# Identity turns that nobody reads, put into TensorE's stops behind conv3, in the end phase and ahead of the first expert tile

## The chip, the cores and the metric

One core of one Trainium2 chip runs the kernel. The metric is the device time of one execution in microseconds (us), and of several runs the median. Profiles come from one execution that the hardware profiler recorded; its span runs from the first to the last instruction.

## The reference, cut to what matters

A residual bottleneck of three convolutions, linear attention, and a mixture of eight experts, all in float32, on 16 images of 256 channels and 14 x 14 pixels (3136 tokens of 256 features).

```python
# 1. convolutions; _bn takes mean and variance over all images and pixels
out = jax.nn.relu(_bn(_conv(x, w1, b1, 1, 0), g1, be1))      # 256 -> 64, 1x1
out = jax.nn.relu(_bn(_conv(out, w2, b2, 1, 1), g2, be2))    # 64 -> 64, 3x3
out = _bn(_conv(out, w3, b3, 1, 0), g3, be3)                 # 64 -> 256, 1x1
x = jax.nn.relu(x + jax.nn.softplus(residual_scale)[0] * out)
t = _to_tokens(x)                                            # (16, 196, 256)
# 2. linear attention on the normalised tokens, 16 heads of 16
q = jax.nn.softmax(q * SCALE, axis=-1); k = jax.nn.softmax(k, axis=-2)
context = jnp.einsum('bnd,bne->bde', q, k)
t = t + jnp.einsum('bde,bnd->bne', context, v).reshape(...) @ w_out + b_out
# 3. experts on the normalised tokens: the two best of eight, weighted
probs = jax.nn.softmax(flat @ gate_w + gate_b, axis=-1)
top_p, top_i = jax.lax.top_k(probs, 2)
for e in range(8):
    h = jax.nn.gelu(flat @ w1[e] + b1[e], approximate=False)  # 256 -> 1024
    out = out + comb[:, e:e + 1] * (h @ w2[e] + b2[e])        # 1024 -> 256
```

The transposes ("turns") that the change adds compute nothing of this: they turn the constant identity matrix, and no instruction reads where they write.

## The kernel before

Every engine has its own instruction list, written by hand in its own block, and runs it in order; engines meet at counted semaphores (`wait_ge(s, n)` waits until semaphore s has reached n). `wait_for(engine, stage, other, name, i)` is such a wait for step `name` of image i. TensorE writes into `ps`, eight banks of 512 float32 columns.

**Convolutions (to about 60 us).** Each layer is computed in 8 chunks of two images (392 columns, `CW`), a chunk per bank. conv3 has two halves of 128 channels, so 16 chunks through 8 banks (L751). Batch norm needs statistics of all chunks before any can go on: VectorE takes them (L1106, counted in `s_st3`), ScalarE copies each chunk behind them into `img` (L533, counted in `s_ca`), and VectorE works out the coefficients (L1038 to L1061). Between conv1 and conv2, and between conv2 and conv3, TensorE runs 22 and 16 products that nobody reads (`spare_products`, L730); they go into columns 392 to 511 of bank `SPARE` (4). Behind conv3 there are none.

**Attention and routing (60 to about 283 us).** A loop over the 16 images runs stages one behind the other: `in` (batch norm and ReLU on VectorE and ScalarE, then `in_turn`, L763, turns the image to tokens by rows), `norm` (statistics, `norm_xT`, L775), `qkv` (L785, L796), `soft`, `ctx`, `out`, `norm2` (L864), gate logits (L874), and for each pair of images the routing on VectorE and `route_rank` on TensorE (L884 to L889), which gives every token its row in its experts' lists. GpSimd scatters the token rows there (L456). The code behind the loop, here the end phase, writes out the last images' steps by hand. There TensorE sums the counts of tokens per expert (L922, L931), VectorE makes from them the table of tiles (L1336 to L1392, its steps counted in `s_tab`), and ScalarE and TensorE wait for parts of it (`TAB_ROWS`, `TAB_EXPERTS`).

**Experts (from about 283 us).** 56 tiles of 128 token rows go through a pipeline over slots. ScalarE loads a tile's rows (`load_rows`, L666); TensorE turns them (`x_turn`, L940); ScalarE and VectorE split them into a leading and a rest part (L672, L1522); TensorE multiplies them by the first matrix in two halves of six products (`hidden`, L947); VectorE adds the bias (L1537), ScalarE takes the GELU (L677); TensorE turns the result (`h_turn`, L974), it is split again (L683, L1516), and TensorE multiplies by the second matrix (`expert_out`, L947). Tiles overlap: in slot m TensorE does `h_turn` of tile m-2, `x_turn` of tile m, `hidden` of tile m-1 and `expert_out` of tile m-2; ScalarE issues the third load of rows only behind the GELU and the copy of the first tiles.

Of the kernel before, what the change touches and what calls it, by code (L numbers as in the profile page):

```python
# [36 lines left out]
CHUNKS = 8  # L37
CW = 2 * HW
# [14 lines left out]
SPARE = 4  # L53
# [27 lines left out]
LAST = B - 1  # L81
# [6 lines left out]
def after(stage, engine, name, i):  # L88

    steps = STEPS[stage][engine]  # L90
    return i * len(steps) + steps.index(name) + 1


def moe_block(nc, x, w1t, w2t, w3t, norms, res_scale, wqkv, wout, bout, gate_w, gate_b, ew1, ew2, eb, out):
# [5 lines left out]
    with ctx:  # L100
        def sb(name, shape, dt=F32):
            return ctx.enter_context(nc.sbuf_tensor(name, shape, dt))

        def sem(name):
            return ctx.enter_context(nc.semaphore(name))
# [15 lines left out]
        ident = sb("ident", [128, 128])  # L121
# [89 lines left out]
        ps = ctx.enter_context(nc.psum_tensor("ps", [128, 8, 512], F32))  # L211
# [11 lines left out]
        s_st3 = sem("conv3_stats")  # L223
        s_fin = sem("conv_coefficients")
        s_ca = sem("conv_applied")
# [43 lines left out]
        def wait_for(eng, stage, engine, name, i):  # L269

            if i >= 0:
                eng.wait_ge(S[stage][engine], after(stage, engine, name, i))
# [441 lines left out]
        def _(pe):  # L714
# [11 lines left out]
            def spare_products(layer, times):  # L726

                pe.wait_ge(s_cst, STATS_READ[layer])
                for _ in range(times):
                    last = pe.matmul(ps[:, SPARE, CW:512], w1s[:, 0, :], img[:, 0, 0:512 - CW], start=True, stop=True)  # L730
                last.then_inc(s_spare, 1)

            pv = pad[:, :].rearrange("p (b r c) -> p b r c", b=B, c=16)
            spare_products(0, 22)
            pe.wait_ge(s_wl, 1)
# [11 lines left out]
            for c in range(CHUNKS):  # L747
                for h in range(2):
                    n = 2 * c + h
                    pe.wait_ge(s_ca, CHUNKS + n + 1 if n < 8 else 2 * CHUNKS + n - 7)  # L750
                    pe.matmul(ps_chunk(n % 8), w3s[:, h * 128:(h + 1) * 128], mid2[:, c * CW:(c + 1) * CW],  # L751
                              start=True, stop=True).then_inc(s_conv, 1)
            pe.wait_ge(s_wa, 9 * 16)
            pe.wait_ge(s_const, NCONST)
            pe.wait_ge(s_ca, 4 * CHUNKS)
# [95 lines left out]
            def norm2_xT(i):  # L851
                wait_for(pe, "norm2", "act", "norm1", i)
                bank = psL
                if i < LAST:
                    wait_for(pe, "gate", "act", "xT", i - 1)
                else:
                    bank = psT
                    wait_for(pe, "ctx", "act", "proj", LAST - 1)

                if i % 2 == 0:  # L860
                    wait_for(pe, "route", "vec", "bias", i // 2 - 1)
                for k in range(2):
                    for j in range(2):
                        last = pe.transpose(bank[:, k * HW + j * HALF:k * HW + (j + 1) * HALF],  # L864
                                            rows[:, i % RING, j, k * 128:(k + 1) * 128], ident[0:HALF, 0:HALF])
                last.then_inc(S["norm2"]["pe"], 1)

            def norm2_logits(i):
                wait_for(pe, "gate", "act", "xT", i)
                wait_for(pe, "route", "vec", "bias", i // 2 - 1)  # L870
                for j in range(2):
                    at = CW + ((i % 2) * 2 + j) * E
                    for k in range(2):
                        last = pe.matmul(psL[0:HALF, at:at + E], xT2[:, i % 2, k, j * HALF:(j + 1) * HALF],  # L874
                                         gw[:, k, :], start=(k == 0), stop=(k == 1))
                last.then_inc(S["gate"]["pe"], 1)

            def route_rank(g):

                both = rt[:, BOTH[g % 2]]  # L880
                wait_for(pe, "route", "vec", "both", g)
                wait_for(pe, "place", "vec", "pos", g - 1)
                wait_for(pe, "norm", "act", "xT", min(2 * g + ROUTE_LAG, B - 1))
                pe.matmul(psX[0:HALF, CW:CW + 32], upper[:, :], both.rearrange("p t e -> p (t e)"),  # L884
                          start=True, stop=False)
                for t in range(3):
                    pe.matmul(psX[0:HALF, CW + (t + 1) * E:CW + 32], ones[:, 0:HALF],
                              both[:, t:t + 1, :].to_broadcast([HALF, 3 - t, E]), start=False, stop=False)
                pe.matmul(psX[0:HALF, CW:CW + 32], ones[:, 0:HALF],  # L889
                          run[:, g % 2, :].unsqueeze(1).to_broadcast([HALF, 4, E]),  # L890
                          start=False, stop=True).then_inc(S["route"]["pe"], 1)
# [30 lines left out]
            pe.matmul(psV[:, E:2 * E], ones[:, :], run[:, (G - 1) % 2, :], start=True, stop=True)  # L922
            norm2_xT(LAST - 2)
            norm2_logits(LAST - 2)
            norm2_xT(LAST - 1)
            norm2_xT(LAST)
            norm2_logits(LAST - 1)
            norm2_logits(LAST)
            route_rank(G - 1)
            wait_for(pe, "route", "vec", "run", G)  # L930
            pe.matmul(psV[:, 0:E], ones[:, :], run[:, (G + 1) % 2, :], start=True, stop=True).then_inc(s_cntp, 1)  # L931
            route_rank(G)

            def x_turn(i, b, late):

                pe.wait_ge(s_xr[b], (i // XR + 1) * 16 if isinstance(i, int) else late)
                if not isinstance(i, int) or i >= 1:
                    pe.wait_ge(s_xlo, i)
                for k in range(2):
                    last = pe.transpose(ps[:, 0, k * 128:(k + 1) * 128], xr[:, b, k * 128:(k + 1) * 128], ident[:, :])  # L940
                last.then_inc(s_eT, 1)
# [42 lines left out]
                         lambda k: off + W2HI + k * C, W2LO - W2HI, C).then_inc(s_yp, 1)  # L984

            pe.wait_ge(s_tab, TAB_EXPERTS)

            def pe_slot(m, b, before=None, e=None, late=None):

                st, p = isinstance(m, int), b % 2  # L990
                if before is None:
                    e = expert_of(m - 1) if 0 <= m - 1 < SLOTS else None
                    before = expert_of(m - 2) if m >= 2 else None
                if not st or 0 <= m - 2 < SLOTS:
                    h_turn(m - 2, p)
                if m == 1:
                    hidden(0, 0, e)
                if not st or m < SLOTS:
                    x_turn(m, b, late)
                if m != 1 and e is not None:  # L1000
                    hidden(m - 1, 1 - p, e)
                if not st or 0 <= m - 2 < SLOTS:
                    expert_out(m - 2, p, before)
# [642 lines left out]
```

## Time and profile before

| | us |
|---|---|
| median of 3 runs | 687.7 (687.45 to 690.37) |
| profiled execution, whole | 689.3 |
| its span, first to last instruction | 687.4 |
| mean granted TensorE clock | 0.947 of full |
| TensorE busy (PE) | 616.8 (90% of the span) |
| VectorE busy (DVE) | 455.4 (66%) |
| ScalarE busy (ACT) | 319.2 (46%) |
| GpSimd busy (POOL) | 218.5 (32%) |

PE stands for TensorE's products and turns, PEld for its weight loads, DVE for VectorE, ACT for ScalarE, POOL for GpSimd, ACTq and SPq for transfers issued by ScalarE and SyncE. L947 is line 947 of the kernel before. A timeline row gives the start, the time, the engine, the line, the operation, what it writes and reads, the number of merged instructions, and in brackets how long the engine had been idle before it and which instruction released it. Busy time of TensorE is modelled at the ends, since its instructions overlap; where something is compared closely, starts are compared with starts. The granted clock is given as a share of 2.4 GHz.

### The profile page before, as it was taken

The page shows a single profiled execution, that of the slowest core. Times are in us where ns is not written, and L with a number is a line of the kernel's source. Part 1 is how long each engine was busy: PE and PEld are TensorE (multiplying, and loading weights), DVE is VectorE, ACT ScalarE, POOL GpSimd, SP SyncE. Part 2 cuts the span into 40 slices and gives each one's busy share as a digit, 9 for nine tenths or more (in the row PEclk, how much of TensorE's full clock was granted, in tenths as well). Part 3 has the DMA queues.
Part 4 walks back from the last instruction along what each step waited for, and adds up shares of the span by engine and source line. Part 5 has one row for each costly group of instructions (what it writes and reads, how often), then busy time and mean ns, then how long its engine had stood idle before and what let it go on. Part 6 is the DMA issues. An engine that isn't in the chain of part 4 may idle for free.

```text
span 687.4 us, 13862 instructions
## 1 busy us (share of the span) xinstructions
PE 616.8 (90%) x3960; PEld 546.7 (80%) x3960; DVE 455.4 (66%) x1472; ACT 319.2 (46%) x624; POOL 218.5 (32%) x194
## 2 busy tenths in 40 slices
PE   7984799989999974489999999999999999999982
PEld 3862678878788864379999999999999999999971
DVE  2877899999998886346565655556565655656550
ACT  0575788888785522133334333333334333333430
POOL 7041233315656667502112222222121222212120
PEclk9996899999999985599999999999999999999995
DMA  9718999888959953422383745626528337222211
GB/s 247 239 62 306 361 351 326 302 293 302 353 201 361 355 182 92 132 45 38 73 289 49 232 131 162 200 44 196 171 35 291 76 99 256 48 44 37 32 17 16
DMA packets 50198, 121.10 MB, mean 176 GB/s; under 512 B 7309, under 2 KB 38865, under 8 KB 43985
## 3 DMA queue, kind: packets, MB, share of 16 engines
q1 hardware_dynamic: 30368, 98.54, 39.8%
q0 software_dynamic: 11136, 14.00, 12.0%
q10 hardware_dynamic: 8624, 7.68, 4.2%
q8 instruction: 39, 0.64, 0.4%
q14 instruction: 31, 0.25, 0.1%
HBM read 68.09 MB, written 52.11 MB: 175 GB/s over the span
## 4 chain that ended last, share of the span: by engine, by line
PE 69%; DVE 20%; issue 4%; ACT 2%; POOL 2%; DMA 1%; DVEq 1%; SPq 0%; ACTq 0%; POOLq 0%
PE ps L947 46%; PE ps L974 7%; DVE wset L1225 3%; DVE stt L1134 2%; PE ps L740 2%; PE ps L722 2%; PE ps L796 2%; PE ps L940 2%; PE ps L751 2%; PE ps L785 1%; PE ps L847 1%; POOL rows_by_expert L456 1%; DVE tc L1125 1%; DVE img L1219 1%; DVE cT L1211 1%
## 5 line engine op out<-in xcount | busy, mean ns | idle before, releaser
L478 POOL DMA_INDIRECT out<-ys,xr x56 | 86.7, 1548 | 302.4 <-DVE ys L1548 220.5
L947 PE MATMUL ps<-wset,hTh 128*128 x896 | 162.7, 282 | 3.4 <-DVE hTl L1516 3.4
L947 PE MATMUL ps<-wset,xrTh 128*128 x448 | 148.7, 414 | 1.2 <-DVE xrTl L1522 1.2
L947 PEld LDWEIGHTS ps<-wset,hTh 128*128 128x128 f32 x896 | 141.6, 190 | 9.7 <-issue 4.8
L677 ACT ACTIVATE hb<-hb 128x512 f32<-128x512 f32 x112 | 70.3, 633 | 138.4 <-DVE hb L1537 133.0
L947 PE MATMUL ps<-wset,hTl 128*128 x448 | 126.1, 281 | 0.0
L683 ACT CAST hTh<-ps 128x512 fp32r<-128x512 f32 x112 | 60.2, 590 | 99.4 <-PE ps L974 99.4
L1543 DVE TENSOR_TENSOR yb<-ps,bset 128x256 f32<-128x256 f32 x56 | 23.8, 425 | 124.5 <-PE ps L947 124.5
L947 PEld LDWEIGHTS ps<-wset,xrTh 128*128 128x128 f32 x448 | 82.0, 193 | 17.7 <-issue 1.6
L947 PE MATMUL ps<-wset,xrTl 128*128 x224 | 90.2, 403 | 0.0
L1537 DVE TENSOR_TENSOR hb<-ps,bset 128x512 f32<-128x512 f32 x112 | 75.4, 684 | 19.7 <-PE ps L947 19.6
L947 PEld LDWEIGHTS ps<-wset,hTl 128*128 128x128 f32 x448 | 85.0, 190 | 0.0
L1516 DVE TENSOR_TENSOR hTl<-ps,hTh 128x512 fp32r<-128x512 f32 x112 | 71.8, 682 | 11.2 <-ACT hTh L683 8.3
L456 POOL DMA_INDIRECT rows_by_expert<-rows,slot x64 | 62.4, 975 | 23.5 <-issue 16.6
L432 POOL TENSOR_TENSOR img<-img,bo 98x512 f32<-98x512 f32 x16 | 29.2, 1828 | 100.2 <-ACT xh L551 96.0
L974 PE MATMUL ps<-ident,hb 128*128 128x128 f32 x448 | 58.2, 273 | 0.7 <-ACT hb L677 0.7
L796 PE MATMUL ps<-xT,wq 128*128 128x196 f32 x256 | 50.1, 339 | 8.9 <-ACT vT L573 8.2
L796 PEld LDWEIGHTS ps<-xT,wq 128*128 128x128 f32 x256 | 43.9, 194 | 14.3 <-ACT xT L568 6.8
L947 PEld LDWEIGHTS ps<-wset,xrTl 128*128 128x128 f32 x224 | 43.1, 193 | 10.5
L974 PEld LDWEIGHTS ps<-ident,hb 128*128 128x128 f32 x448 | 50.3, 141 | 0.9 <-ACT hb L677 0.9
L940 PE MATMUL ps<-ident,xr 128*128 128x128 f32 x112 | 22.1, 280 | 13.3 <-DMA xr<-rows_by_expert 13.3
L1225 DVE TENSOR_TENSOR wset<-wset 128x2048 fp32r<-128x2048 f32 x14 | 31.9, 2281 | 0.0
(199 smaller groups left out, 945.8 us busy)
## 6 DMA issues: line engine op xcount, KB each, us to landing
split_weights<-wset SPq DMA_DIRECT2D x16, 2048.0 KB, 7.4
wset<-split_weights SPq DMA_DIRECT2D x32, 1024.0 KB
wset<-in_ew SPq DMA_DIRECT2D x16, 1024.0 KB, 10.5
xr<-rows_by_expert ACTq DMA_DIRECT2D x56, 132.5 KB, 2.3
bset<-in_eb SPq DMA_DIRECT2D x8, 640.0 KB
out<-img SPq DMA_DIRECT2D x16, 196.0 KB
img<-in_x SPq DMA_DIRECT2D x6, 392.0 KB, 7.2
rows_by_expert<-padrow SPq DMA_DIRECT2D x9, 132.5 KB, 3.3
```

The costliest lines, as they stand in the source:

```text
L432: pool.tensor_tensor(t, t, bo2[:, :, :].rearrange("p j d -> p (j d)"), ALU.add).then_inc(S["norm"]["pool"], 1)
L456: pool.indirect_dma_start(norm_rows, bass.IndirectOffsetOnAxis(slot[:, g % 2, k, t:t + 1], 0), rows[:, at, h, :], None).then_inc(s_rows[g ...
L478: pool.indirect_dma_start(out, bass.IndirectOffsetOnAxis(xr[:, r % XR, C + E:ROW].bitcast(U32), 0), ys[:, r % YS, :], None, compute_op=ALU ...
L677: act.activation(hb[:, p, h * 512:(h + 1) * 512], hb[:, p, h * 512:(h + 1) * 512], ACT.Gelu).then_inc(s_ge, 1)
L683: act.copy(hTh[:, p, h * 512:(h + 1) * 512], ps[:, 3 + h, :]).then_inc(s_hhi, 1)
L796: last = pe.matmul(dst[:, h * HW:(h + 1) * HW], wq[:, k, off + h * 128:off + (h + 1) * 128], xT[:, p, k, :], start=(k == 0), stop=(k == 1))
L940: last = pe.transpose(ps[:, 0, k * 128:(k + 1) * 128], xr[:, b, k * 128:(k + 1) * 128], ident[:, :])
L947: last = pe.matmul(dst, rows_k[:, k * 128:(k + 1) * 128], wset[:, bass.ds(column(k) + rest, width)], start=(k == 0 and n == 0), stop=(k == ...
L974: last = pe.transpose(ps[:, 3 + h, k * 128:(k + 1) * 128], hb[:, p, h * 512 + k * 128:h * 512 + (k + 1) * 128], ident[:, :])
L1225: V.tensor_tensor(part_lo[a], raw[u % RAWS], part_hi[a].bitcast(F32), ALU.subtract).then_inc(s_lo_vec, 1)
L1516: V.tensor_tensor(hTl[:, p, part], ps[:, 3 + h, :], hTh[:, p, part].bitcast(F32), ALU.subtract).then_inc(s_hlo, 1)
L1537: V.tensor_tensor(hb[:, p, h * 512:(h + 1) * 512], ps[:, 1 + h, :], bset[:, bass.ds(off + h * 512, 512)], ALU.add).then_inc(s_hb, 1)
```

## The change

Twenty-four turns of the identity behind conv3, after a wait for the chunk of conv3 that used their bank last; eight behind the gate logits of image LAST-2 (behind a wait for the step that last read their bank, 6), eight behind the last rank but one, ten behind the last rank, all into bank 6; and thirty-two into bank 6 behind the wait for the tile table, ahead of the first `x_turn`. Each turn is one transpose of 128 x 128 float32 with the identity as both operands; nothing else is altered, and no order of any engine's other instructions. The lines of the changed kernel stand 5 to 13 later than those of the kernel before.

```diff
@@ -730,6 +730,11 @@
                     last = pe.matmul(ps[:, SPARE, CW:512], w1s[:, 0, :], img[:, 0, 0:512 - CW], start=True, stop=True)
                 last.then_inc(s_spare, 1)
 
+            def spare_turns(bank, times):
+
+                for _ in range(times):
+                    pe.transpose(ps[:, bank, CW - 8:CW + 120], ident[:, :], ident[:, :])
+
             pv = pad[:, :].rearrange("p (b r c) -> p b r c", b=B, c=16)
             spare_products(0, 22)
             pe.wait_ge(s_wl, 1)
@@ -750,6 +755,9 @@
                     pe.wait_ge(s_ca, CHUNKS + n + 1 if n < 8 else 2 * CHUNKS + n - 7)
                     pe.matmul(ps_chunk(n % 8), w3s[:, h * 128:(h + 1) * 128], mid2[:, c * CW:(c + 1) * CW],
                               start=True, stop=True).then_inc(s_conv, 1)
+            pe.wait_ge(s_st3, 2 * CHUNKS - 4 + 1)
+            pe.wait_ge(s_ca, 2 * CHUNKS + 2 * CHUNKS - 4 + 1)
+            spare_turns(SPARE, 24)
             pe.wait_ge(s_wa, 9 * 16)
             pe.wait_ge(s_const, NCONST)
             pe.wait_ge(s_ca, 4 * CHUNKS)
@@ -922,14 +930,18 @@
             pe.matmul(psV[:, E:2 * E], ones[:, :], run[:, (G - 1) % 2, :], start=True, stop=True)
             norm2_xT(LAST - 2)
             norm2_logits(LAST - 2)
+            wait_for(pe, "out", "vec", "add", LAST - 1)
+            spare_turns(6, 8)
             norm2_xT(LAST - 1)
             norm2_xT(LAST)
             norm2_logits(LAST - 1)
             norm2_logits(LAST)
             route_rank(G - 1)
+            spare_turns(6, 8)
             wait_for(pe, "route", "vec", "run", G)
             pe.matmul(psV[:, 0:E], ones[:, :], run[:, (G + 1) % 2, :], start=True, stop=True).then_inc(s_cntp, 1)
             route_rank(G)
+            spare_turns(6, 10)
 
             def x_turn(i, b, late):
 
@@ -984,6 +996,7 @@
                          lambda k: off + W2HI + k * C, W2LO - W2HI, C).then_inc(s_yp, 1)
 
             pe.wait_ge(s_tab, TAB_EXPERTS)
+            spare_turns(6, 32)
 
             def pe_slot(m, b, before=None, e=None, late=None):
 
```

## Rows read from the trace of the kernel before

**Rows 1.** The page's row of granted clock by 40 slices; the chain that ended last.

```profile
PEclk9996899999999985599999999999999999999995
...
PE 69%; DVE 20%; issue 4%; ACT 2%; POOL 2%; DMA 1%; DVEq 1%; SPq 0%; ACTq 0%; POOLq 0%
```

**Rows 2.** TensorE's waits from 300 us on: waited for, us in total, times, longest us.

```profile
PE ps L947 <- DVE hTl L1516: 3.4, 3, 2.1
```

**Rows 3.** Stretches: us, PE busy (instructions), granted clock, DMA share, GB/s.

```profile
58.00:59.00 1.00, 0.00 (x0) 0.55 1.28 484
...
77.61:80.46 2.85, 0.00 (x0) 1.00 1.10 419
...
256.00:257.00 1.00, 0.64 (x6) 0.54 0.08 28
...
259.35:263.70 4.35, 4.29 (x25) 0.50 0.24 72
...
290.00:291.00 1.00, 0.77 (x6) 0.90 0.00 0
...
293.00:294.00 1.00, 0.54 (x3) 0.81 0.51 139
...
297.00:298.00 1.00, 1.00 (x6) 0.98 0.00 0
```

**Rows 4.** TensorE's timeline at full clock: start, us, line, idle before in brackets.

```profile
300.95 1.04 PE L974 MATMUL ps<-ident,hb 128*128 128x128 f32 x8
301.82 0.38 PE L940 MATMUL ps<-ident,xr 128*128 128x128 f32 x2
301.96 0.71 PE L947 MATMUL ps<-wset,xrTh 128*128 x2
...
304.62 0.40 PE L947 MATMUL ps<-wset,xrTl 128*128 x1
```

**Rows 5.** Timelines of ScalarE and TensorE behind conv3.

```profile
54.15 0.49 ACT L533 COPY img<-ps 128x392 f32<-128x392 f32 x1 [0.17 <-DVE bst L1106]
...
54.66 0.82 PE L751 MATMUL ps<-mid,w3s 128*128 128x392 f32 x2
60.99 1.06 PE L763 MATMUL ps<-ident,tc 128*98 128x128 f32 x4 [5.51 <-ACT tc L540]
...
75.34 0.60 PE L763 MATMUL ps<-ident,tc 128*98 128x128 f32 x4
```

**Rows 6.** TensorE's timeline, end phase and first expert tiles.

```profile
259.35 1.90 PE L864 MATMUL ps<-ident,rows 98*128 98x98 f32 x8 [2.70 <-ACT rows L551]
...
268.32 0.59 PE L931 MATMUL ps<-run,ones 98*128 98x8 f32 x2 [2.86 <-DVE run L1301]
...
270.10 0.52 PE L889 MATMUL ps<-run,ones 98*98 98x32 f32 x2
282.58 0.66 PE L940 MATMUL ps<-ident,xr 128*128 128x128 f32 x2 [11.95 <-DMA xr<-rows_by_expert]
284.42 1.21 PE L947 MATMUL ps<-wset,xrTh 128*128 x2 [1.18 <-DVE xrTl L1522]
...
289.27 0.63 PE L947 MATMUL ps<-wset,xrTl 128*128 x1
...
293.46 0.57 PE L940 MATMUL ps<-ident,xr 128*128 128x128 f32 x2 [1.34 <-DMA xr<-rows_by_expert]
```

**Rows 7.** All engines' timeline, from the routing's end to the first tiles.

```profile
263.80 0.19 DVE L1250 TENSOR_TENSOR rt<-ps,gb 98x32 f32<-98x32 f32 x1 [0.71 <-PE ps L874]
...
265.50 0.19 DVE L1312 TENSOR_TENSOR rt<-ps,expert_row 98x32 f32<-98x32 f32 x1 [0.59 <-PE ps L889]
...
276.60 0.20 DVE L1392 CAST tbi<-tb 128x64 int32<-128x64 f32 x1
...
279.18 0.35 ACTq L666 DMA_DIRECT2D xr<-rows_by_expert  x1
...
291.31 1.29 ACTq L666 DMA_DIRECT2D xr<-rows_by_expert  x2
```

## The prediction

> **What bounds the kernel now.** I read the page's row of granted clock first, then the chain that ended last, then TensorE's timeline around each place of the change, and last its waits in the expert phase. TensorE sets the end: 69% of the chain is its work [rows 1]. Its clock is nearly always at 2.4 GHz; of the 40 slices those below 9 are the fourth and fifth (52 to 86 us), the fifteenth to seventeenth (241 to 292) and the last [rows 1]. From 300 us to the end TensorE waits 3.4 us in all, three times, for VectorE's rest part of the turned hidden rows [rows 2]; the rest of these 375 us is back-to-back products. So microseconds won ahead of 300 us arrive at the end of the kernel, unless a wait that is hidden today comes up.
>
> The clock by stretch [rows 3]: it falls to the half level (1.2 GHz) just after 58 us, when conv3 is over, and is full again in the turns at 75.34 [rows 5]. It falls just after 256 us and stays at half until about 290.2; it falls again between 293 and 294 and is full from 297 on [rows 3]. A stop's length alone does not settle it: TensorE stood still for 2.85 us from 77.61 and kept the full clock [rows 3], while behind conv3 it had lost it some 2.6 us after its last product [rows 3, 5]. So the moment of the change is not the program's alone, and the same stop can cost more or less from one execution to the next.
>
> **The change, part by part.** The four places only add turns of a 128x128 identity, 82 in all. The price of one at full clock: eight turns at L974 fill 300.95 to the next line's start at 301.82, so 0.109 us each [rows 4]. At half clock I take twice that, 0.218.
>
> *Behind conv3, 24 turns.* The waits ahead of them are for the chunk whose bank they write, the fourth from last, once its statistics and its copy are over; ScalarE makes the copy behind the statistics, at 54.15, and is done at 54.64, while TensorE's last products end at 55.48 [rows 5]. So neither wait holds anything. The turns end near 55.5 + 24 x 0.109 = 58.1, at half clock near 60.7; TensorE is next wanted at 60.99, for in_turn(0) [rows 5]. The stop of 5.51 us hides them; without it they would cost 2.6. What they can give: in_turn(0) takes 1.06 us at half clock and 0.60 at full [rows 5], and VectorE's and ScalarE's steps to the next turns follow from it, so 0.46 us. The stops behind it hold no new turns, and I leave what follows as it is. Ends: 0 and 0.46; I take 0.46.
>
> *End phase, 8 + 8 + 10 turns.* At half clock they need 1.7, 1.7 and 2.2 us. The first eight stand in the stop of 2.70 us before 259.35, the second eight in the stop of 2.86 us before 268.32, the ten behind the rank that ends at 270.62 [rows 6], where the wait for the tile table follows, which VectorE's cast ends at 276.8 [rows 7]. So none delays anything. Do they hold the clock? It falls at about 256.1 today, ahead of the first of them, and in 259.35 to 263.70 TensorE's rows are busy for 4.29 of 4.35 us without bringing it back [rows 3]; that stretch begins with eight turns of 98 columns [rows 6], and products of 8 columns follow. Eight turns at full clock are 0.87 us in a stop of 2.7. I take 0; the other end is rival B.
>
> *Ahead of the first expert tile, 32 turns.* They start once the tile table is there, 276.8 + some 0.1 us. TensorE stands idle then until the first rows land, at 282.58 [rows 6], and their load at 279.18 is ScalarE's and waits for the same table [rows 7], not for TensorE. All at half clock they take 7.0 us, to 283.9, 1.3 too late. With k of them at half clock and the rest at full they end at 276.9 + 3.49 + 0.109 k, which is 282.58 at k = 20. So if the clock is back within 4.4 us of turning, nothing is late. It came back today at 290.2, behind products that began at 284.42, and at about 297.0, behind products that began soon after 293.46 [rows 3, 6], 5.8 and 3.3 us later. I count no delay as the likelier end and keep 1.3 as the other.
>
> What a full clock then gives. x_turn(0) takes 0.66 us at half and 0.38 at full: 0.28 less [rows 4, 6]. The twelve products of tile 0 last from 284.42 to the last one's start at 289.27, 4.85 us; the same twelve at full clock last from 301.96 to 304.62, 2.66; with the last product's own 0.2 that is 2.4 less [rows 4, 6]. The way on to tile 1 hangs on it in one line: VectorE's bias, ScalarE's GELU, behind it on ScalarE's queue the third load of rows at 291.31 [rows 7], and TensorE waits for those rows until 293.46 [rows 6]. So all 2.7 us move forward. Tile 1's products run at half clock from about 293.8 to 297.0 [rows 3], 3.2 us that full clock would do in 1.6: 1.6 more, if the clock survives the stops between. Today it does not, and no turns are put there; I take 0 and keep 1.6 for the range. What is late next is VectorE's rest part of [rows 2]; it follows tile 1's products and moves with them.
>
> **The sum.** The profiled execution took 689.3 us (the span of 687.4 and 1.9 around it): 689.3 - 0.46 - 2.7 = 686.1. It stands 1.6 above the median of 687.7 (687.45 to 690.37). I do not take these 1.6 off as well: an execution whose clock comes back earlier in tile 0 has less to win there, so from the median I expect about 1.7 and not 3.2. I say **686.0**, 0.25% below the median. About 0.5%, 3.4 us, is what a measurement of this kernel can tell from no change, so the forecast lies inside it.
>
> **The rivals.** *A, the turns neither hold the clock nor bring it back.* For it: in 259.35 to 263.70 the rows were busy throughout, eight turns among them, and the clock stayed at half [rows 3, 6]. Against it: the kernel already has products nobody reads, at L730 between the conv layers, and the clock is full there until 58 us [rows 1, 3]; but those are products, not turns. In this case nothing is won, the 32 turns end at 283.9, and x_turn(0), with every tile behind it, is 1.3 us later: 687.7 + 1.3 = 689.0, slower than before. It decides as soon as more than 20 of the 32 run at half clock. Chance 0.30.
>
> The Trainium skill, in "TensorE: Matmul & The Clock Gate", section "Part 4: PE-mode transpose", says that the full clock does not engage for transposes, since they do not count as busy in the same way. By that rule rival A is the whole result, 689.0 in place of 686.0. No row here is a stretch of turns alone, so the trace of before neither bears it out nor refutes it.
>
> *B, the clock is held through the end phase too.* TensorE's lateness there lies on VectorE's path: 0.71 us before L1250 and 0.59 before L1312 [rows 7]; the last count and rank take from 268.32 to 270.62 [rows 6], 2.3 us, of which full clock would save half, 1.15. The tile table and the first load come 2.45 us sooner: 686.1 - 2.45 = 683.6, and 682.0 with tile 1 at full clock as well. Against it: the 26 turns are 2.8 us at full clock in a stretch of 20, and the fall comes ahead of them. Chance 0.10.
>
> *C, what is won at tile 0 is given back.* The stops between tile 0 and tile 1 stay (1.34 us before 293.46 [rows 6]), and a clock that is back sooner can also fall sooner. Then tile 1 starts earlier, but its 2.66 us of products run wholly at half clock, 2.6 lost in place of 1.6; and a median run, with perhaps 1.2 of the 2.7 to win, wins 0.2: 687.5. Chance 0.12.
>
> The forecast has the rest, 0.48.
>
> **How the numbers follow.** The low end is the median less all of conv3 and tile 0, 687.7 - 3.2 = 684.5, and some of tile 1's 1.6: 683.8. The high end is rival A, 689.0. Outside lie most of B and the tails. Faster by over 0.5% (below 684.3): most of B and the luckiest of the forecast, 0.12. Slower by over 0.5% (above 691.1): no mechanism here reaches it, 0.03 for what I have not seen. Within: 0.85.
>
> **What would show it.** In the profile after, the 24 turns should end near 58 and in_turn(0) take 0.60 and not 1.06. The clock should still be at half from about 257. The 32 turns should begin near 277 and stand 0.21 apart at first and 0.109 later; that change of spacing, and the granted clock of the stretch, part the forecast from rival A. x_turn(0) should start near 282.6, and the twelve products behind it last 2.7 and not 4.85. If x_turn(0) starts well before 282, the end phase was won too (B). If tile 0 is fast but the time from its products to tile 2's is as long as today or longer, C holds. A median above 687.5 or below 684 makes the forecast wrong.

## The result, and the profile after

The changed kernel takes 690.9 us (median of 20 runs, 687.02 to 693.29), the kernel before 688.29 (20 runs, 686.53 to 693.9). The ratio of the runs is 1.003, with a 95% interval of 1.0017 to 1.0044: **slower by 0.3%, some 2.1 us** (1.2 to 3.0; the medians stand 2.6 apart). The forecast was 686.0 with a range up to 689.0, so both its sign and its range were wrong; that the difference stays within 0.5% was right.

The profiled execution of the changed kernel took 693.29 us, 2.4 above its median and the slowest of its 20; that of before took 689.3, 1.0 above its own. The two traces differ by more than the medians do, and not all of it is the change's, as will be seen.

The page of the kernel after, its row of granted clock and the shares of the chain that ended last, which answer to [rows 1]:

```profile
PEclk9998699999999995789999999999999999999995
...
PE 67%; DVE 21%; issue 4%; ACT 3%; DMA 2%; SPq 1%; DVEq 1%; POOL 0%; ACTq 0%; POOLq 0%
```

One-microsecond stretches of the kernel after (stretch, us, TensorE busy and instructions, granted clock, DMA share, GB/s), as in [rows 3]:

```profile
46.00:47.00 1.00, 1.00 (x3) 0.55 0.00 0
...
63.00:64.00 1.00, 0.93 (x4) 0.58 0.76 320
...
261.00:262.00 1.00, 0.00 (x0) 0.57 0.00 0
284.00:285.00 1.00, 1.00 (x7) 0.50 0.91 233
285.00:286.00 1.00, 1.00 (x11) 0.99 0.50 158
294.00:295.00 1.00, 1.00 (x8) 1.00 0.00 0
295.00:296.00 1.00, 0.00 (x0) 0.64 0.54 136
...
301.00:302.00 1.00, 1.00 (x4) 0.50 0.00 0
302.00:303.00 1.00, 1.00 (x10) 0.95 0.00 0
```

TensorE's timeline after; L736 are the added turns, L771 is `in_turn`, L952 `x_turn`, L959 the products and L986 `h_turn`. It answers to [rows 5] and [rows 6]:

```profile
57.33 2.78 PE L736 MATMUL ps<-ident 128*128 128x128 f32 x24
63.01 0.93 PE L771 MATMUL ps<-ident,tc 128*98 128x128 f32 x4 [2.89 <-ACT tc L540]
...
259.33 1.07 PE L736 MATMUL ps<-ident 128*128 128x128 f32 x8
...
274.26 2.38 PE L736 MATMUL ps<-ident 128*128 128x128 f32 x10
280.66 5.82 PE L736 MATMUL ps<-ident 128*128 128x128 f32 x32 [4.03 <-DVE tbi L1405]
286.84 0.44 PE L952 MATMUL ps<-ident,xr 128*128 128x128 f32 x2 [0.35 <-DMA xr<-rows_by_expert]
288.45 0.73 PE L959 MATMUL ps<-wset,xrTh 128*128 x2 [1.18 <-DVE xrTl L1535]
...
289.72 0.39 PE L959 MATMUL ps<-wset,xrTl 128*128 x1
...
291.13 0.40 PE L959 MATMUL ps<-wset,xrTl 128*128 x1
...
293.75 1.25 PE L986 MATMUL ps<-ident,hb 128*128 128x128 f32 x8 [2.00 <-ACT hb L677]
296.32 0.69 PE L952 MATMUL ps<-ident,xr 128*128 128x128 f32 x2 [1.33 <-DMA xr<-rows_by_expert]
296.66 1.21 PE L959 MATMUL ps<-wset,xrTh 128*128 x2
...
301.51 0.63 PE L959 MATMUL ps<-wset,xrTl 128*128 x1
...
309.88 0.50 PE L959 MATMUL ps<-wset,hTh 128*128 x2 [0.94 <-DVE hTl L1529]
```

Three things are to be seen. The clock comes back at 285.02, inside the 32 turns, and x_turn(0) waits for its rows and not for the turns. Tile 0's twelve products are fast: 288.45 to the last start at 291.13, 2.68 us where it was 4.85 [rows 6]. But TensorE then stands still for 2.00 us ahead of h_turn and for 1.33 ahead of x_turn(2), the turn of the third tile, tile 2; the clock falls at 295.28, and tile 1's products, 296.66 to 301.51, run wholly at half: 4.85 us.

Why the fast products brought so little stands on VectorE's timeline. First after, then before, each from the rest part of tile 0 (`xrTl`) to the bias (`hb`; before with the last product of half 0 and the bias of half 1):

```profile
287.78 0.42 DVE L1535 TENSOR_TENSOR xrTl<-ps,xrTh 128x256 fp32r<-128x256 f32 x1 [7.18 <-ACT xrTh L672]
288.18 0.19 DVE L1410 COPY tb<-tb 128x56 f32<-128x56 f32 x1
...
290.83 0.16 DVE L1573 TENSOR_REDUCE meta<-wsel 128x1 f32<-128x8 f32 x1
292.34 1.29 DVE L1550 TENSOR_TENSOR hb<-ps,bset 128x512 f32<-128x512 f32 x2 [1.35 <-PE ps L959]
```

```profile
283.75 0.42 DVE L1522 TENSOR_TENSOR xrTl<-ps,xrTh 128x256 fp32r<-128x256 f32 x1 [6.96 <-ACT xrTh L672]
...
286.71 0.63 PE L947 MATMUL ps<-wset,xrTl 128*128 x1
...
286.82 0.16 DVE L1560 TENSOR_REDUCE meta<-wsel 128x1 f32<-128x8 f32 x1
288.32 0.69 DVE L1537 TENSOR_TENSOR hb<-ps,bset 128x512 f32<-128x512 f32 x1 [1.35 <-PE ps L947]
...
290.05 0.69 DVE L1537 TENSOR_TENSOR hb<-ps,bset 128x512 f32<-128x512 f32 x1 [1.03 <-PE ps L947]
```

From rest part to bias it is 4.56 us after and 4.57 before. Between them VectorE builds schedule tables (L1410 to L1427) that its code puts into slot 0. The rows name TensorE as what ended the last 1.35 us, but the last product of half 0 started at 289.72 and took 0.39, so TensorE had been done for 2.2 us: what binds is VectorE's own queue. In these 1.35 us the code has VectorE read two entries of the tile table into registers (`expert_of`), which the profile does not count as busy; that they fill the time is not shown by a run. For the first bias the queue bound before, too: that half's last product started at 286.71 and took 0.63, and the bias came 1.0 us behind its end, where in table_early and x32_table below, with the tables out of the way, it comes 0.26 behind it. The second bias, at 290.05, did wait for its products before (the last started at 289.27 [rows 6]). After, both halves are waiting when VectorE gets there (x2, one block of 1.29 us).

So in this pair of traces the way from rest part to x_turn(2) is 8.54 us (287.78 to 296.32) where it was 9.71 (283.75 to 293.46): 1.17 won. From x_turn(2) to tile 1's second matrix it is 13.56 (296.32 to 309.88) where it was 12.40 (293.46 to 305.86): 1.16 lost. Behind that nothing differs in this pair: from tile 1's second matrix to the end it is 381.62 us after and 381.54 before, and the wait of [rows 2] is again 3.4 us in three parts. The rest of the 4.1 us between the two spans lies ahead of the first load of rows (283.00 against 279.18 [rows 7]); 1.7 of it in conv3, where this execution lost the clock at 46.1 in the middle of products. That is ahead of every added turn. Of the other 2.1, 1.0 lies in the attention, where the clock falls again at 83.6, and 0.8 between the gate logits of image LAST-2 and the first load. table_early, a kernel below without any turns, has all three in its trace too (falls at 45.1 and 82.6, and 0.7 more than before behind the logits), so they are no price of the turns; the recorded execution of before was spared them.

### The profile page after: what moved, and what is told of

It reads as the page before. It is cut to its first block, busy times and chain, and to the rows that moved or that the text cites. A ratio compares the mean times of both kernels' runs of the same rounds, so it can differ in the third digit from the quotient of the medians.

```text
span 691.5 us, 14026 instructions
## 1 busy us (share of the span) xinstructions
PE 631.0 (91%) x4042; PEld 559.1 (81%) x4042; DVE 454.9 (66%) x1472; ACT 319.7 (46%) x624; POOL 218.7 (32%) x194
## 4 chain that ended last, share of the span: by engine, by line
PE 67%; DVE 21%; issue 4%; ACT 3%; DMA 2%; SPq 1%; DVEq 1%; POOL 0%; ACTq 0%; POOLq 0%
PE ps L959 45%; PE ps L986 7%; DVE wset L1238 3%; DVE stt L1147 2%; PE ps L745 2%; PE ps L804 2%; PE ps L952 2%; PE ps L756 2%; PE ps L793 2%; PE ps L722 1%; DVE img L1232 1%; DVE cT L1224 1%; DVE tc L1138 1%; DMA img<-in_x 1%; DVE qr L1209 1%
## 5 line engine op out<-in xcount | busy, mean ns | idle before, releaser
L959 PE MATMUL ps<-wset,hTh 128*128 x896 | 163.0, 283 | 3.4 <-DVE hTl L1529 3.4
L959 PEld LDWEIGHTS ps<-wset,hTh 128*128 128x128 f32 x896 | 141.8, 190 | 9.9 <-issue 5.1
L959 PE MATMUL ps<-wset,xrTh 128*128 x448 | 147.6, 411 | 1.2 <-DVE xrTl L1535 1.2
L959 PE MATMUL ps<-wset,hTl 128*128 x448 | 126.3, 282 | 0.0
L959 PEld LDWEIGHTS ps<-wset,xrTh 128*128 128x128 f32 x448 | 81.2, 191 | 17.2 <-issue 1.4
L959 PE MATMUL ps<-wset,xrTl 128*128 x224 | 89.5, 400 | 0.0
L959 PEld LDWEIGHTS ps<-wset,hTl 128*128 128x128 f32 x448 | 85.2, 190 | 0.0
L986 PE MATMUL ps<-ident,hb 128*128 128x128 f32 x448 | 58.2, 273 | 2.0 <-ACT hb L677 2.0
L986 PEld LDWEIGHTS ps<-ident,hb 128*128 128x128 f32 x448 | 50.2, 140 | 2.4 <-ACT hb L677 2.4
L959 PEld LDWEIGHTS ps<-wset,xrTl 128*128 128x128 f32 x224 | 42.8, 191 | 10.4
L793 PE MATMUL ps<-wq,xT 128*98 128x256 f32 x128 | 32.6, 400 | 0.0
```

What stands on the lines that cost most here:

```text
L793: last = pe.matmul(psQ[0:HALF, j * C:(j + 1) * C], xT[:, p, k, j * HALF:(j + 1) * HALF], wq[:, k, 0:C], start=(k == 0), stop=(k == 1))
L959: last = pe.matmul(dst, rows_k[:, k * 128:(k + 1) * 128], wset[:, bass.ds(column(k) + rest, width)], start=(k == 0 and n == 0), stop=(k == ...
L986: last = pe.transpose(ps[:, 3 + h, k * 128:(k + 1) * 128], hb[:, p, h * 512 + k * 128:h * 512 + (k + 1) * 128], ident[:, :])
```

## The experiments

The theories, with the letters that the expectations use for them. **V**: the 32 turns cost the time; VectorE's tables keep the won microseconds from reaching tile 1, and the clock, back early, falls again ahead of tile 1. **S**: it is the turns behind conv3. **E**: it is the turns of the end phase. **D**: the 32 turns hold x_turn back. **T**: the tables are the whole of it. **I**: only the parts together cost it. Several expectations missed, those of V too; each is answered behind its numbers.

Each kernel has 12 runs, beside 35 runs of the kernel before on the same chip (medians 688.48, 688.38 and 688.45 for the three groups). "Phase" is the time from the first load of rows to tile 1's second matrix in the kernel's own trace, 26.68 us in the trace before (279.18 to 305.86) and 26.88 after (283.00 to 309.88). "Clock" says when it is back to full there, and when it falls again.

**First group: the parts alone, and the tables alone.**

c3_only has the 24 turns behind conv3 and no others.

```diff
+            pe.wait_ge(s_st3, 2 * CHUNKS - 4 + 1)
+            pe.wait_ge(s_ca, 2 * CHUNKS + 2 * CHUNKS - 4 + 1)
+            spare_turns(SPARE, 24)
             pe.wait_ge(s_wa, 9 * 16)
```

> Only the 24 turns behind conv3. Theory V (the loss is at the first expert tiles: the 32 turns bring the clock back, but the first bias of tile 0 waits for VectorE's own tables, 4.57 us behind its rest part in both traces, and the clock falls again ahead of tile 1): 0 to 0.5 us below the kernel before, in_turn(0) often at 0.6 us. Theory S (the conv3 turns move the clock's later falls into the attention stage, as the fall at 83.6 us in the changed kernel's profile, which cost 1.2 us): 1 to 2 us above.

Median 687.97, ratio 0.9981 (0.9961 to 1.0002); phase 24.55, clock back at 290.84 and not lost again. S falls, by these runs and by the traces: the fall in the attention that it blames on these turns (83.6) stands also in end_only, x32_only and table_early (82.0 to 82.6), which have no turns behind conv3. The turns end near 59.6 and in_turn(0) takes 1.06 us, as without them.

end_only has the 8 + 8 + 10 turns of the end phase.

```diff
             norm2_logits(LAST - 2)
+            wait_for(pe, "out", "vec", "add", LAST - 1)
+            spare_turns(6, 8)
...
             route_rank(G - 1)
+            spare_turns(6, 8)
...
             route_rank(G)
+            spare_turns(6, 10)
```

> Only the 8 + 8 + 10 turns of the end phase. Theory V: within 0.4 us of the kernel before, clock at half from about 257 us to the expert tiles. Theory S: the same. A third theory, E (turns at half clock push the routing chain): 1 us or more above, with the tile table later against the logits than the 21.0 us (255.58 to 276.60) of before.

Median 687.67, ratio 0.9983 (0.9964 to 1.0003); phase 24.78, clock back at 290.68 and kept. E falls too: the tile table comes 21.71 us behind the logits, in c3_only, without these turns, 21.69. The median is 0.8 below before, more than the 0.4 that V and S allowed.

x32_only has the 32 turns ahead of the first tile.

```diff
             pe.wait_ge(s_tab, TAB_EXPERTS)
+            spare_turns(6, 32)
```

> Only the 32 turns ahead of the first expert tile. Theory V: 1 to 2 us above the kernel before, the first bias of tile 0 again some 4.5 us behind VectorE's rest part, tile 1's products at half clock throughout. Theory S and theory E: within 0.5 us of the kernel before, or below it.

Median 689.93, ratio 1.0015 (0.9996 to 1.0033); phase 26.61. The clock is back at 283.36, inside the turns, and falls at 293.6; x_turn(0) waits 0.25 us for its rows behind the turns, so D falls. Rest part to first bias takes 4.52 us, tile 1's products are at half clock. Against before the interval reaches 1; on the same chip its mean is 2.67 us above that of end_only (95%: 1.67 to 3.67), 2.17 above c3_only's (1.1 to 3.2) and 1.61 above table_early's (0.6 to 2.6).

table_early has no turns; VectorE builds the schedule tables before tile 0 and not in slot 0.

```diff
             drain(chains[1])
-            dve.wait_ge(s_tab, TAB_EXPERTS)
+            drain(schedule_table())
...
-                if m == 0:
-                    drain(schedule_table())
...
```

> The kernel before, with VectorE's schedule tables (seven steps, 2.4 us) made right behind the tile table, in its idle time of 7 us ahead of tile 0's rest part, and not behind that part. No turns. Theory V: VectorE is free when tile 0's first half is done, the bias follows the products, 0.5 to 1.5 us below the kernel before. If the bias waits for the products anyway (the rival), within 0.3 us.

Median 688.32, ratio 0.9999 (0.9981 to 1.0016); phase 24.59. Without turns tile 0's products are at half clock and bind themselves: the bias waits 3.16 us for TensorE, and VectorE's time is no loss. So the rival came true, and V's gain of 0.5 to 1.5 us did not.

**Second group: the two halves of V.**

x32_gap keeps the clock up between tile 0 and tile 1 with more turns that nobody reads.

```diff
+            spare_turns(6, 32)
...
+                if m == 2:
+                    spare_turns(6, 10)
                 if not st or m < SLOTS:
                     x_turn(m, b, late)
+                if m == 1:
+                    spare_turns(6, 14)
```

> The 32 turns alone, and 14 more turns behind tile 1's x_turn and 10 more behind tile 0's h_turn, in the two stops of 2.0 and 1.4 us in which the clock fell in the profiles of the change and of x32_only. Theory V (what costs is that the clock falls ahead of tile 1, whose products then run at half clock): the clock stays full from before tile 0 on, the time from the first load of rows to expert_out's first product of tile 1 is 24 us or less and not 26.6, the median 1 to 2 us below the kernel before, some 3 below x32_only. Rival D (the 32 turns cost by holding back the first x_turn): the stop's turns change nothing, 1 to 2 us above the kernel before, as x32_only.

Median 688.39, ratio 0.9997 (0.9979 to 1.0015); phase 23.71. The clock is back at 279.56 and stays. The stops of 2.00 and 1.33 us are now 0.48 and 0.22. Rest part to bias is still 4.61. The phase is what V forecast; the median, the same as before's, is neither V's 1 to 2 below nor D's 1 to 2 above. The recorded execution, 684.32, is the fastest of its twelve.

x32_table has the 32 turns and the tables ahead of tile 0.

```diff
+            spare_turns(6, 32)
...
-            dve.wait_ge(s_tab, TAB_EXPERTS)
+            drain(schedule_table())
...
```

> The 32 turns alone, with VectorE's schedule tables made in its idle time ahead of tile 0. Theory V: the first bias of tile 0 comes some 3.3 us behind VectorE's rest part and not 4.57, and everything to tile 1's rows moves by up to 1.2 us; the stops get shorter, but if the clock still falls in them the median stays above the one of table_early, at 688.5 to 689.5. Rival T (VectorE's tables are all of the loss): the median is 1.2 us or more below table_early, at 687 or less.

Median 688.15, ratio 0.9992 (0.9973 to 1.0011); phase 24.07. Rest part to bias is 2.60 us, so the tables were what hid the win: from rest part to x_turn(2) it is 7.46 us, against 8.53 in table_early, 1.07 won. But the clock falls at 293.56 and is back only at 297.0, and from x_turn(2) to tile 1's second matrix it takes 12.51 us against 11.00: 1.5 lost. That speaks against T, by which nothing would be lost behind the tables, and the median is above T's 687; it is also below V's 688.5 to 689.5. So the tables have a part: with them out of the way the 32 turns no longer show a loss against before, though tile 1 still pays.

table_loads has no turns, the tables early, and the second and third load of rows right behind the first.

```diff
             load_rows(0, 0)
+            load_rows(1, 1)
+            load_rows(2, 2)
             turned(0, 0)
-            load_rows(1, 1)
...
-            load_rows(2, 2)
...
+            drain(schedule_table())
...
```

> No turns. Tables early, and ScalarE's loads of rows for tiles 1 and 2 issued right behind the first, not behind the first GELU. The wait of 1.3 us for tile 2's rows should go; at half clock in tile 0 the products bind. Expected some 1 us below the kernel before, 687.2 to 687.8; if the wait for the rows only gives way to the wait for VectorE, no difference.

Median 688.25, ratio 0.9993 (0.9977 to 1.0008); phase 23.70. The stop ahead of x_turn(2) shrinks from 1.20 to 0.22 us; of the 0.9 us that the phase is shorter than in table_early the median shows nothing beyond its interval, and the 1 us that was expected did not come.

turns78_table_loads adds to that 78 turns behind the last rank, in one row.

```diff
             route_rank(G)
+            wait_for(pe, "out", "vec", "add", LAST - 1)
+            spare_turns(6, 78)
```

> table_loads with 78 turns behind the last rank, not behind the tile table, so that the clock is full when the first rows land, and with no stop left between tile 0 and tile 2 in which it could fall. Theory V: full clock from tile 0 on, 21 to 22 us from the first load to expert_out's first product of tile 1, and a median 3 to 4 us below the kernel before, 684.5 to 685.5. If turns ahead of tile 0 cost as such (rival D), no lower than table_loads.

Median **686.95**, ratio 0.9981 (0.9966 to 0.9997): the one version of twelve whose interval lies below the kernel before, and by little; it also beats the change. Phase 22.72. Against table_loads on the same chip its mean is 1.35 us lower (0.21 to 2.49). V had forecast 684.5 to 685.5, by a full clock from tile 0 on. Its stretches show that the clock comes back in the turns and falls again in the middle of tile 0's products:

```profile
275.00:276.00 1.00, 1.00 (x7) 0.50 0.21 57
276.00:277.00 1.00, 1.00 (x7) 0.60 0.94 278
286.00:287.00 1.00, 1.00 (x5) 1.00 0.40 126
287.00:288.00 1.00, 1.00 (x4) 0.52 0.35 104
290.00:291.00 1.00, 1.00 (x7) 0.77 0.28 83
```

**Third group: the change with and without its 32 turns, on one chip.**

change_again is the changed kernel once more, with no edit; the next kernel leaves out the second of these lines:

```diff
             pe.wait_ge(s_tab, TAB_EXPERTS)
             spare_turns(6, 32)
```

> The change itself once more, on the same chip as the three below. Theory V, with the parts measured so far (conv3 -0.5, end phase -0.9, the 32 turns +1.6 us in the mean): 0 to 1 us above the kernel before. A theory I (the parts act on each other, as the 2.1 us of the first comparison say): about 2 us above.

Median 690.35, ratio 1.0026 (1.0011 to 1.0041): the loss is there again. Phase 26.73. This is the number of I (about 2 above) and not of V (0 to 1 above): what c3_only and end_only seemed to win does not simply come off the loss of x32_only.

c3_end is the change without the 32.

```diff
             pe.wait_ge(s_tab, TAB_EXPERTS)
-            spare_turns(6, 32)
```

> The change without its 32 turns. Theory V: the sum of the two parts, 0.5 to 1.5 us below the kernel before, and 2 us or more below the change itself. Theory I: less than 0.5 us below the kernel before, or above it.

Median 688.1, ratio 0.999 (0.997 to 1.0009); phase 24.84. Between these two kernels stand only the 32 turns: means 690.32 and 688.12, **2.2 us** (1.07 to 3.33), phases 1.89 us apart. The 2 us below the change are V's; the 0.35 below before are I's (less than 0.5), not V's 0.5 to 1.5. Their traces, c3_end first: the first load, TensorE's x_turn(0), VectorE's rest part, x_turn(2) and the first product of tile 1's second matrix, and then the stretches.

```profile
280.99 0.35 ACTq L666 DMA_DIRECT2D xr<-rows_by_expert  x1
...
284.94 0.66 PE L952 MATMUL ps<-ident,xr 128*128 128x128 f32 x2 [10.29 <-DMA xr<-rows_by_expert]
...
286.11 0.42 DVE L1534 TENSOR_TENSOR xrTl<-ps,xrTh 128x256 fp32r<-128x256 f32 x1 [7.48 <-ACT xrTh L672]
...
294.85 0.44 PE L952 MATMUL ps<-ident,xr 128*128 128x128 f32 x2 [1.34 <-DMA xr<-rows_by_expert]
...
305.83 0.50 PE L959 MATMUL ps<-wset,hTh 128*128 x2 [0.86 <-DVE hTl L1528]
```

```profile
288.00:289.00 1.00, 1.00 (x3) 0.50 0.45 132
289.00:290.00 1.00, 1.00 (x4) 0.62 0.35 101
...
293.00:294.00 1.00, 0.51 (x4) 1.00 0.25 30
295.00:296.00 1.00, 1.00 (x6) 1.00 0.24 82
...
671.00:672.00 1.00, 1.00 (x10) 1.00 0.31 46
```

And change_again, the same rows:

```profile
278.16 5.77 PE L736 MATMUL ps<-ident 128*128 128x128 f32 x32 [4.03 <-DVE tbi L1405]
...
280.51 0.35 ACTq L666 DMA_DIRECT2D xr<-rows_by_expert  x1
...
284.29 0.44 PE L952 MATMUL ps<-ident,xr 128*128 128x128 f32 x2 [0.37 <-DMA xr<-rows_by_expert]
...
285.24 0.42 DVE L1535 TENSOR_TENSOR xrTl<-ps,xrTh 128x256 fp32r<-128x256 f32 x1 [7.14 <-ACT xrTh L672]
...
293.88 0.69 PE L952 MATMUL ps<-ident,xr 128*128 128x128 f32 x2 [1.38 <-DMA xr<-rows_by_expert]
...
307.24 0.60 PE L959 MATMUL ps<-wset,hTh 128*128 x2 [0.85 <-DVE hTl L1529]
```

```profile
282.00:283.00 1.00, 1.00 (x10) 0.79 0.78 232
...
292.00:293.00 1.00, 0.50 (x4) 0.83 0.29 36
293.00:294.00 1.00, 0.12 (x1) 0.50 0.58 143
295.00:296.00 1.00, 1.00 (x3) 0.50 0.00 0
...
672.00:673.00 1.00, 1.00 (x7) 0.50 0.51 77
```

Here the account of the first tiles is in two sums. From the first load (280.99 and 280.51) to x_turn(2): 13.86 us without the 32 turns and 13.37 with them, 0.49 won (0.39 of it ahead of VectorE's rest part, by a shorter x_turn(0) and rows that landed sooner). From x_turn(2) to tile 1's second matrix: 10.98 without and 13.36 with them, 2.38 lost. In the end 1.89 us are lost there, near the 2.2 of the runs.

The two spans stand 2.8 us apart, though (688.7 and 685.9). change_again is 0.48 earlier at the first load, and behind tile 1 it takes 1.39 us longer. That lies in the last tile: TensorE stops for 2.07 us ahead of its second matrix in both, and in change_again the clock falls in the products behind that stop, at 671.5, while in c3_end it stays (the last stretch of each). The same fall stands in eight of the fourteen traces, those of before and after among them: in five of six with the 32 turns, in three of eight without. So one trace of a kernel can be 1.4 us off by it, and whether the turns make it more frequent, and so have a share of the 2.2 there, is not shown.

change_gap is the change with the 14 and 10 turns of x32_gap.

```diff
+                if m == 2:
+                    spare_turns(6, 10)
                 if not st or m < SLOTS:
                     x_turn(m, b, late)
+                if m == 1:
+                    spare_turns(6, 14)
```

> The change with 14 more turns behind tile 1's x_turn and 10 more behind tile 0's h_turn, as in x32_gap. Theory V: the clock is full from before tile 0 on, and the median is 2 us or more below the change itself and at or below the kernel before. Theory I: above the kernel before, like the change.

Median 688.39, ratio 1.0006 (0.9988 to 1.0023); phase 24.33. Only the stops between the two tiles are filled; x_turn(2) to tile 1's second matrix takes 10.95 us and not 13.36, and the mean is 1.48 us (0.43 to 2.53) below change_again. V's 2 us or more below the change came out as 1.96 in the medians. The last tile has no part in this pair of traces: from tile 1's second matrix to the end each takes 381.46 us. So the clock's fall in those stops carries the loss, or most of it, and T, as the whole, falls, since the tables still stand in slot 0 here. I, as the only cause, falls too: the change without the 32 stands at before's time, and x32_only alone lies above the three kernels beside it and shows the same trace as the change. But how the other turns add to that is open.

best joins the turns behind conv3, the two eights, 78 turns behind the last rank, ten behind x_turn(0), the tables and the loads early.

```diff
             route_rank(G)
-            spare_turns(6, 10)
+            spare_turns(6, 78)
...
-            spare_turns(6, 32)
...
                     x_turn(m, b, late)
+                if m == 0:
+                    spare_turns(6, 10)
...
+            load_rows(2, 2)
...
+            drain(schedule_table())
...
```

> The conv3 turns, 8 + 8 turns in the end phase, 78 turns behind the last rank in place of 10 and of the 32, 10 turns between tile 0's x_turn and its products, VectorE's schedule tables early, and ScalarE's loads for tiles 1 and 2 behind the first. Theory V: full clock from tile 0 on, 21 to 22 us from the first load to expert_out's first product of tile 1, and 2.5 to 4 us below the kernel before. If the turns of conv3 or of the end phase cost something in this company (theory I), no lower than the 1.4 us below of turns78_table_loads.

Median 687.57, ratio 0.998 (0.9955 to 1.0004); phase 23.92. Not resolved from before, not V's 2.5 to 4 below, and no better than turns78_table_loads, which is what theory I put. Here the 78 turns end at 281.96 and x_turn(0) starts at 284.59, behind 2.63 us of standing still; the clock, back at 275.16, falls at 285.4, and is back at 288.8.

## Why the prediction was wrong

By its own steps:

- *Behind conv3, "I take 0.46".* Too much. In the profile after, in_turn(0) takes 0.93 and not 0.60 us, in c3_only, c3_end and change_again 1.06 [rows 5]. The turns do put off the stop, but 2.9 us of it remain ahead of in_turn(0), and the clock falls there or within in_turn(0). By the runs of c3_only the gain is between none and 2.7 us, so what these turns give stays open; the step's own row shows nothing.
- *End phase, "I take 0".* Right as far as seen. The clock falls at 261.1 and not at 256.1; the first eight turns run at full clock (1.07 us) and the ten at half (2.38), and the half level holds until the 32. Since this execution was late by then, the fall is better counted from the start of the gate logits of LAST-2: 2.5 us behind it after (258.62), 0.5 before (255.58), but 2.4 in table_early, which has no turns there. So the turns did not visibly hold the clock. Nor did they delay anything: the tile table's cast stands 21.8 us behind the logits, in table_early 21.7.
- *Ahead of the first tile, "no delay".* Right. The clock is back 4.36 us after the first of the 32 (280.66 to 285.02), just under the 4.4 that the sum allowed; the rows come later. Rival A, that turns neither hold the clock nor bring it back, is refuted: in x32_only, change_again, change_gap and x32_gap it came back 3.1 to 4.3 us after the first of the 32, with nothing else on TensorE.
- *"The way on to tile 1 hangs on it in one line ... So all 2.7 us move forward."* **The first step that failed.** The line leaves out VectorE's queue: 2.8 us of tables and row sums and 1.35 behind them stand between the rest part and the first bias. In the recorded execution of before the second bias still waited for TensorE, and there 1.17 of the 2.7 arrive; once the products are faster, the queue binds both biases. And 2.7 was too much for a usual execution, whose clock comes back within tile 0: its products up to x_turn(1) take 4.24 us in c3_end and 2.90 in change_again, 1.34 won. From rest part to x_turn(2) that leaves 8.74 and 8.64: 0.10 of the 1.34 arrives. With the tables out of the way, 1.07 of 1.37 does (table_early against x32_table).
- *"1.6 more, if the clock survives the stops ... I take 0."* **The step that made the sign.** I read the stretch 293 to 297 at half clock [rows 3] as the state of the kernel before. Of the traces of kernels with neither the 32 turns nor the 78, five of six (c3_only, end_only, table_early, table_loads, c3_end) lose no clock there: it comes back late in tile 0, at 289.8 to 290.8, and is there for tile 1. The one recorded execution of before is the sixth. Bringing it back earlier lost it at 295.28, 293.6 and 292.66 (the change, x32_only, change_again), so tile 1 paid 2.4 that it usually does not pay. The term's low end should have been a loss of 2.2, the price of tile 1's products at half clock (4.85 against 2.66).
- *Rival C* named this, with a chance of 0.12, but set what tile 1 can lose at 2.6 against 1.6 "today"; it came out at 687.5 for the same reason.
- The text did say that an execution whose clock comes back earlier in tile 0 has less to win there. It did not ask what such an execution stands to lose behind it.

Against the trace the Trainium skill's rule on transposes ("TensorE: Matmul & The Clock Gate", section "Part 4: PE-mode transpose"), that the full clock does not engage for them, does not hold for these float32 turns: the stretches 284 to 286 above go from 0.50 to 0.99 with turns alone. By that rule the loss would have been x_turn(0) held back by 1.3 us; it was not held back, and the loss came from tile 1.

That the kernel before is usually in the better of the two courses is an inference from five traces and from the medians; before itself was recorded once. That filling the stops and moving the tables together would turn the loss into a gain was not run with the 32 turns; turns78_table_loads and best, which come nearest, lost the clock in tile 0 (287.04) or just ahead of its products (285.4). What the turns behind conv3 and in the end phase are worth, each within an interval that reaches 1, stays open, and so do what sets the exact moment of a fall and what the last tile has to do with it.

## What to carry to other kernels

Warming TensorE up early is only worth what the stops behind it leave: price the next busy stretch at half clock as a loss that may be new, and fill the stops up to the last one before steady work, or leave the warm-up out (here filling them took the loss away and won nothing against before). When an engine is to become faster, add up what stands in the queue of the engine that takes its result, and compare the releaser that a row names with the end of that engine's work. And a state of the clock in one profiled execution is a draw, not the rule; a term that rests on it needs both values.

## What was not expected of the hardware

Turns of the identity alone bring the clock from 1.2 to 2.4 GHz: in x32_gap after 3.1 us of them (276.49 to 279.56). The clock also falls while TensorE is busy: in turns78_table_loads at 287.04, inside tile 0's back-to-back products, 1.2 us after they began at 285.87 behind stops of 0.75 and 1.18 us, and in the kernel after at 46.1, inside conv3's, 1.1 us after they began at 45.03 behind a stop of 2.02. So a fall need not lie inside a stop; which stop it answers to is not shown.
